# A two-layer graph kernel on one core: where the ones of a row are counted, and when the verdict on the inputs falls

## The reference: what is computed

```python
adj0 = A * (y @ y.T)                              # layer 0: neighbours of the same class
adj0 = adj0 / max(sum(abs(adj0), axis=1), 1e-12)
x = layernorm(x + 0.9 * (adj0 @ x) + 0.1 * h0)
sim = tanh(adj * adj) * (adj > 0)                 # layer 1: tanh(1) at every one
new_adj = top_350_of_each_row(sim)                # all of it where a row has at most 350 ones
feat = relu(new_adj @ (tanh(x @ W_proj + b_proj) @ W_gcn) + b_gcn)
out = layernorm(x + feat)
```

## Time and profile before

| | |
|---|---|
| median of 3 runs | 478.86 us (477.89 to 480.38) |
| profiled execution, its own time | 478.8 us |
| its span, first to last instruction | 477.0 us |
| PE busy | 449.3 us, 94% |
| DVE busy | 378.9 us, 79% |
| ACT busy | 262.7 us, 55% |
| transfers | 108.50 MB, 418 GB/s in layer 0, under 20 GB/s in layer 1 |

### The profile page before, as it was taken

One profiled execution on the slowest core, in us unless ns is written; L12 is line 12 of the kernel. 1 busy time (PEld: TensorE's weight loads), 2 busy tenths in 40 slices (PEclk: granted clock), 3 DMA queues, 4 the chain that ended last, 5 costly groups with the idle time before them and its releaser, 6 DMA issues.

```text
span 477.0 us, 15332 instructions
## 1 busy us (share of the span) xinstructions
PE 449.3 (94%) x5104; PEld 391.1 (82%) x5104; DVE 378.9 (79%) x1401; ACT 262.7 (55%) x353; POOL 159.5 (33%) x309
## 2 busy tenths in 40 slices
PE   3669999999999999999999999999999999999990
PEld 2448888989998899889998878888888888888880
DVE  5889999999999999999999866566566566566552
ACT  4988999999999999999999826300000000000000
POOL 3012544445555554444555431221221221221220
PEclk9988999999999999999999999999999999999996
DMA  8999999999999999999998000000000000000000
GB/s 267 406 419 418 402 419 393 384 416 417 414 416 416 421 418 422 420 419 421 419 415 326 8 0 1 19 11 17 17 11 17 17 11 17 17 11 17 17 18 10
DMA packets 28254, 108.50 MB, mean 227 GB/s; under 512 B 5401, under 2 KB 18226, under 8 KB 18226
## 3 DMA queue, kind: packets, MB, share of 16 engines
q1 hardware_dynamic: 28226, 108.14, 56.6%
HBM read 105.57 MB, written 2.56 MB: 227 GB/s over the span
## 4 chain that ended last, share of the span: by engine, by line
PE 88%; DVE 5%; DMA 2%; issue 2%; ACT 1%; POOL 1%; POOLq 0%; DVEq 0%; SPq 0%; ACTq 0%
PE acc L492 73%; PE words L443 8%; PE proj_acc L571 3%; PE feat_acc L555 2%; DMA a_rows<-in_adj_dram 2%; DVE a_bits L746 2%; PE xnt_acc L547 1%; DVE g_words L302 1%; POOL pack_half L373 1%; DVE turned L830 1%; ACT count_out L648 1%; DVE x_parts L775 0%; PE gram_acc L475 0%; DVE y_diag L760 0%; DVE same_class L850 0%
## 5 line engine op out<-in xcount | busy, mean ns | idle before, releaser
L492 PE MATMUL acc<-x_parts,turned 128*128 128x257 f16 (+1 forms) x1600 | 195.8, 277 | 0.7 <-DVE x_parts L775 0.7
L648 ACT ACTIVATE count_out<-a_rows,ones 128x2688 bf16<-128x2688 f32 (+1 forms) x80 | 190.0, 2375 | 0.5
L492 PEld LDWEIGHTS acc<-x_parts,turned 128*128 128x128 fp8e4 (+1 forms) x1600 | 157.0, 99 | 25.9 <-DVE x_parts L775 1.2
L492 PE MATMUL acc<-f_parts,turned 128*128 128x257 f16 (+1 forms) x1560 | 175.4, 273 | 0.0
L492 PEld LDWEIGHTS acc<-f_parts,turned 128*128 128x128 fp8e4 (+1 forms) x1560 | 151.2, 97 | 23.2 <-issue 0.4
L746 DVE TENSOR_SCALAR a_bits<-a_rows 128x2688 bf16<-128x2688 f32 (+1 forms) x80 | 116.7, 1459 | 3.3 <-DMA a_rows<-in_adj_dram 2.9
L830 DVE TENSOR_SCALAR turned<-a_words 128x320 uint16 (+1 forms) x305 | 66.9, 233 | 58.7 <-PE acc L492 58.4
L400 POOL TENSOR_TENSOR var_eps<-mean_var,consts 128x1 f32<-128x1 f32 x80 | 18.5, 231 | 272.6 <-DVE mean_var L1036 143.2
L403 POOL TENSOR_TENSOR rstd<-var_eps,consts 128x1 f32<-128x1 f32 x80 | 86.0, 1075 | 6.3
L830 DVE TENSOR_SCALAR turned<-same_class 128x320 uint16<-128x320 uint16 x313 | 71.2, 253 | 0.1
L443 PEld LDWEIGHTS words<-pack,a_bits 128*128 128x128 bf16 (+1 forms) x1600 | 53.6, 96 | 10.3 <-DVE a_bits L746 6.7
(11 more groups left out here) (109 smaller groups left out, 289.9 us busy)
## 6 DMA issues: line engine op xcount, KB each, us to landing
a_rows<-in_adj_dram SPq DMA_DIRECT2D x39, 1344.0 KB, 8.1
a_rows<-in_adj_dram SPq DMA_DIRECT2D x39, 1156.0 KB, 8.6
h_rows<-in_L_gnn_h_dram SPq DMA_DIRECT2D x39, 64.0 KB, 6.1
out_dram<-xn SPq DMA_DIRECT2D x39, 64.0 KB, 1.5
xs<-in_x_dram SPq DMA_DIRECT2D x3, 640.0 KB, 10.0
xs<-in_x_dram SPq DMA_DIRECT2D x1, 512.0 KB, 9.0
y_nat<-in_L_gnn_y_dram SPq DMA_DIRECT2D x1, 304.0 KB, 3.6
a_rows<-in_adj_dram SPq DMA_DIRECT2D x1, 84.0 KB
```

The lines of the kernel that those rows point to most:

```text
L492: mm = pe.matmul(acc[par][0:m, 0:PARTS], bits, parts[:, b, 0:PARTS], start=first and b == blocks[0], stop=last and b == blocks[-1])
L648: act.activation(count_out[0:m, 0:w], a_rows[par][h][0:m, 0:w], ACT.Relu, bias=ones[0:m, 0:1], scale=-HUGE, accum_out=col).then_inc(s_coun ...
```

## The change

1. `pack` gets a ninth column of ones. Packing a block of `a_bits` then gives 8 words and the number of ones. Results lie 10 apart (`PITCH`) in PSUM and in `a_words`, 9 of each 10 are copied by ACT. The readers of `a_words` on DVE (mask, unpack of layer 1) now read 8 of each 10.
2. `f_parts` loses its constant column: rows of 256 columns, 256 apart, and layer 1 multiplies 256 columns. `x_parts` keeps 257. The reading of `degree` in every block of layer 1 is gone.
3. The check changes: ACT sums all ones of a partition over the whole of `a_words` in one instruction behind its other checks; DVE sums `need` over the blocks and compares the two totals. These checks move to steps 3 and 4 of layer 1 on DVE (in `before`: step 39 and behind the last block).
4. PE's matmul of the verdict stands ahead of the products of the last row block, the flag is written in DVE's step NB, ahead of the last block's output.
5. Both paths share one block of code: no barrier between them. Each engine waits for the flag, loads it and branches. SP's wait for the stores moves behind its branch. Where the general path runs, the five engines meet at a semaphore first.

The core of the diff:

```diff
+    PITCH = WORDS + 2
-        pack = sb("pack", [P, WORDS], BF16)
+        pack = sb("pack", [P, WORDS + 1], BF16)
-        f_parts = sb("f_parts", [P, NB, PARTS + 1], F16)
-        a_words = sb("a_words", [P, NB, NB * WORDS], U16)
+        f_parts = sb("f_parts", [P, NB, 2 * F], F16)
+        a_words = sb("a_words", [P, NB, NB * PITCH], U16)
...
             steps(sp, store, 0)
-            sp.wait_ge(s_out[0], 16 * (NB // 2))
-            sp.wait_ge(s_out[1], 16 * (NB // 2))
...
-                    mm = pe.matmul(words[par][0:k, b * WORDS:(b + 1) * WORDS],
+                    mm = pe.matmul(words[par][0:k, b * PITCH:b * PITCH + WORDS + 1],
                                    a_bits[h][0:m, c:c + (k - 1) * d + 1:d], pack[0:m, :], start=True, stop=True)
...
             def multiply_blocks(n, par, m, parts, blocks, first=False, last=False):
+                cols = PARTS if parts is x_parts else 2 * F
                 for b in blocks:
                     bits = turned_at(n, par)[:, b, :].bitcast(F8)[:, 0:m]
-                    mm = pe.matmul(acc[par][0:m, 0:PARTS], bits, parts[:, b, 0:PARTS],
+                    mm = pe.matmul(acc[par][0:m, 0:cols], bits, parts[:, b, 0:cols],
                                    start=first and b == blocks[0], stop=last and b == blocks[-1])
...
+                if isinstance(t, int) and t == LAST:
+                    pe.wait_ge(s_good, CHECKS)
+                    pe.matmul(feat_acc[0:1, 0:1], verdict[:, :], ones[:, 0:1], start=True, stop=True)\
+                        .then_inc(s_sum, 1)
...
-                    act.activation(at(a_words, n, P), words[par][:, 0:NB * WORDS], ACT.Copy).then_inc(s_words, 1)
+                    act.activation(at(a_words, n, P).rearrange("p (b w) -> p b w", w=PITCH)[:, :, 0:WORDS + 1],
+                                   words[par][:, 0:NB * PITCH].rearrange("p (b w) -> p b w", w=PITCH)[:, :, 0:WORDS + 1],
+                                   ACT.Copy).then_inc(s_words, 1)
...
+            act.wait_ge(s_measured, 4)
+            act.activation(count_out[:, 0:NB * NB].rearrange("p (n b) -> p n b", b=NB),
+                           a_words[:, :, :].rearrange("p n (b w) -> p n b w", w=PITCH)[:, :, :, WORDS],
+                           ACT.Copy, accum_out=ones_in[:, :]).then_inc(s_measured, 1)
...
+            dve.memset(pack[:, WORDS:WORDS + 1], 1.0)
...
+            def check_sums():
+                dve.wait_ge(s_measured, 5)
+                done(dve.tensor_scalar(holds[:, 3, :], x_sums[:, :], 1.0, None, ALU.is_le))
+                done(dve.tensor_scalar(holds[:, 4, :], f_sums[:, :], 1.0, None, ALU.is_le))
+                done(dve.tensor_reduce(good[:, :], holds[:, :, :], AX.XY, ALU.min))
+                done(dve.tensor_tensor(surplus[:, :], ones_in[:, :], need_in[:, :], ALU.subtract))
+                done(dve.scalar_tensor_tensor(verdict[:, :], good[:, :], 1.0, surplus[:, :], ALU.subtract, ALU.add))
...
+            def words_at(n):
+                return at(a_words, n, P).rearrange("p (b w) -> p b w", w=PITCH)[:, :, 0:WORDS]
...
-                    dve.tensor_scalar(degree[0:m, bass.ds(t - 2, 1)], acc[par][0:m, 2 * F:PARTS], 0.5 / SCALE,
-                                      None, ALU.mult).then_inc(s_degree, 1)
...
+                if isinstance(t, int) and t == 3:
+                    check_counts()
+                if isinstance(t, int) and t == 4:
+                    check_sums()
+                if isinstance(t, int) and t == NB:
+                    dve.wait_ge(s_sum, 1)
+                    dve.tensor_scalar(flag[:, :], feat_acc[0:1, 0:1], 0.0, 0.0, ALU.is_equal, ALU.is_equal)\
+                        .then_inc(s_flag, 1)
...
+            pe.wait_ge(s_flag, 1)
             bad = pe.value_load(flag[0:1, 0:1], min_val=0, max_val=1)
             with pe.If(bad != 0):
+                pe.sem_inc(s_quit, 1)
+                pe.wait_ge(s_quit, 5)
...
+            sp.wait_ge(s_stored[0], 16 * (NB // 2))
+            sp.wait_ge(s_stored[1], 16 * (NB // 2))
```

More of the change, by code:

```diff
@@ L34, with packed_path @@
 PART_MAX = 32768.0
-def packed_path(nc, x, adj, h0, y, w_proj, b_proj, w_gcn, b_gcn, out, flag):
+def packed_path(nc, engines, sem, x, adj, h0, y, w_proj, b_proj, w_gcn, b_gcn, out, flag, s_flag, s_out):
     N, F = x.shape
@@ L52, in packed_path @@
     PARTS = 2 * F + 1
-    CHECKS = 11
+    CHECKS = 13
+    PITCH = WORDS + 2
     EARLY = NB - 4
@@ L58, in packed_path @@
     assert F == P and 0 < TAIL <= 2 * WORDS and C == BITS and FULL % 4 == 3 and FULL > FIRST
-    assert NB * WORDS <= 512 and NB % 4 == 0
+    assert NB * PITCH <= 512 and NB % 4 == 0
     def rows_of(t):
@@ L180, in packed_path @@
         zeros_in = sb("zeros_in", [P, 2 * NB])
-        degree = sb("degree", [P, NB])
+        ones_in = sb("ones_in", [P, 1])
+        need_in = sb("need_in", [P, 1])
+        surplus = sb("surplus", [P, 1])
+        verdict = sb("verdict", [P, 1])
         x_sums = sb("x_sums", [P, NB])
@@ L263, in packed_path @@
         s_passed = sem("s_passed")
-        s_degree = sem("s_degree")
         s_result = sem("s_result")
-        s_out = [sem(f"s_out{p}") for p in range(2)]
         s_good = sem("s_good")
         s_sum = sem("s_sum")
-        s_flag = sem("s_flag")
         def turned_at(n, par):
@@ L459, in _ @@
                 mm = pe.matmul(y_pack[b // Y_CUT][:, c:c + WORDS],
-                               y_masked[:, b, :], pack[:, :], start=True, stop=True)
+                               y_masked[:, b, :], pack[:, 0:WORDS], start=True, stop=True)
                 if b in (Y_CUT - 1, LAST):
@@ L603, in _ @@
             steps(pe, step1, 0)
-            pe.wait_ge(s_good, CHECKS)
-            pe.matmul(feat_acc[0:1, 0:1], good[:, :], ones[:, 0:1], start=True, stop=True)\
-                .then_inc(s_sum, 1)
         @engines.scalar
@@ L726, in _ @@
             for p in range(2):
-                dve.memset(words[p][:, LAST * WORDS:NB * WORDS], 0.0)
+                dve.memset(words[p][:, LAST * PITCH:NB * PITCH], 0.0)
             dve.memset(zeros_in[:, :], N / 2)
-            for a in (degree, x_sums, f_sums):
+            for a in (x_sums, f_sums):
                 dve.memset(a[:, :], 0.0)
             dve.memset(x_parts[:, :, 2 * F], SCALE)
-            dve.memset(a_words[:, LAST, LAST * WORDS:NB * WORDS], 0).then_inc(s_cleared, 1)
+            dve.memset(a_words[:, LAST, LAST * PITCH:NB * PITCH], 0).then_inc(s_cleared, 1)
             dve.memset(y_diag[:, :, :, :], 0.0).then_inc(s_yp_sb, 1)
             dve.wait_ge(s_pack, BITS)
-            dve.tensor_tensor(pack[:, :], pack_half[:, 0, :], pack_half[:, 1, :], ALU.add).then_inc(s_packs, 1)
+            dve.memset(pack[:, WORDS:WORDS + 1], 1.0)
+            dve.tensor_tensor(pack[:, 0:WORDS], pack_half[:, 0, :], pack_half[:, 1, :], ALU.add).then_inc(s_packs, 1)
             dve.tensor_reduce(in_half[:, :], pack_half[:, :, :], AX.X, ALU.max).then_inc(s_packs, 1)
@@ L762, in _ @@
             dve.wait_ge(s_yp_sb, TURN + 1)
-            dve.memset(words[1][:, LAST * WORDS:NB * WORDS], 0.0).then_inc(s_yp_sb, 1)
+            dve.memset(words[1][:, LAST * PITCH:NB * PITCH], 0.0).then_inc(s_yp_sb, 1)
             cast(0, 0, 0, 0)
@@ L782, in feature_ones @@
             def feature_ones():
-                dve.memset(f_parts[:, LAST, 0:2 * F], 0.0)
-                dve.memset(f_parts[:, :, 2 * F], SCALE).then_inc(s_cleared, 1)
+                dve.memset(f_parts[:, LAST, :], 0.0).then_inc(s_cleared, 1)
             k = [0]
@@ L940, in bits @@
                     if valid(t - 1):
-                        unpack(t - 1, odd, rows_of(t - 1), same_class[:, :], lo, hi)
+                        unpack(t - 1, odd, rows_of(t - 1), same_class[:, :].rearrange("p (b w) -> p b w", w=WORDS), lo, hi)
                 def begin(t_of, u, lo, hi):
                     if isinstance(t, int) and t == t_of:
-                        unpack(u + NB, u % 2, rows_of(u), at(a_words, u, P), lo, hi)
+                        unpack(u + NB, u % 2, rows_of(u), words_at(u), lo, hi)
                 begin(NB + 3, 1, 0, BITS // 2)
@@ L999, in bits @@
                     if valid(t) and (not isinstance(t, int) or t > 2):
-                        unpack(t + NB, par, rows_of(t), at(a_words, t, P), lo, hi)
+                        unpack(t + NB, par, rows_of(t), words_at(t), lo, hi)
                 bits(0, 2)
@@ L1155, in block_view @@
             return a[0:FULL * P, :].rearrange("(b p) f -> p b f", p=P)
-        block = ctx.enter_context(nc.Block())
         def row_range(t, m):
@@ L1462, in gnn_kernel, with sem @@
 def gnn_kernel(nc, x, adj, h0, y, w_proj, b_proj, w_gcn, b_gcn, out):
-    with nc.sbuf_tensor("flag", [1, 1], I32) as flag:
-        packed_path(nc, x, adj, h0, y, w_proj, b_proj, w_gcn, b_gcn, out, flag)
-        general_path(nc, x, adj, h0, y, w_proj, b_proj, w_gcn, b_gcn, out, flag)
+    with nc.sbuf_tensor("flag", [1, 1], I32) as flag, ExitStack() as sems, nc.Block() as engines:
+        def sem(name):
```

(5 more changed lines are left out.)

54 lines of the change are left out of this document (29 added, 25 removed).

## The result

| | before | changed |
|---|---|---|
| median, on one chip | 478.86 us (477.89 to 480.38, 5 runs) | 471.02 us (470.71 to 472.29, 5 runs) |
| ratio, 95% interval | | 0.984, 0.982 to 0.986 |
| profiled execution: time, span | 478.8, 477.0 us | 470.7, 468.9 us |

A forecast was written before the change was run, and what follows sets the result against it. PE was taken to bound both layers, in layer 0 with DVE and ACT close behind. From 478.8 us, -5.2 (tail), -5.0 (layer 1 products), +0.1 and +0.2 gave 468.9 us; range for 8 in 10: 467.2 to 473.4.

The forecast's parts named there:

- main case: Whole kernel: all four parts work as forecast, 468.9 us, own range 467.6 to 470.4; chance 0.72.
- rival of another late branch: End of the kernel: DVE's branch takes 3.85 us and delays the barrier, +2.6 us, 471.5 us; chance 0.11.
- signs of being wrong: Mask or unpack over 400 ns, layer 0 grown, or more than 0.5 us between the store's landing and the barrier.
- Part 1: The tail: all but the last store's landing and one barrier leaves the path, span ends at 471.8, -5.2 us.
- 470.1, if its branch stays short: End of the kernel: DVE's finish time in us, from output ready at 469.1, 0.9 for the flag, 0.07 for its branch.
- Part 2: Layer 1 products with 256 columns: 3.2 ns less each over 1560 products, -5.0 us.
- columns only: Layer 1: a product becomes only 0.42 ns shorter, -0.65 us, time 473.2 us; chance 0.12.
- Part 3: Layer 0: ninth packing column free on PE, ACT's copy and DVE's mask hidden; memsets at the start cost +0.1 us.
- rival that ended slower: Layer 1: DVE's unpack, reading 8 of each 10, loses the fast mode, 412 to 490 ns, time 482.9 us; chance 0.04.
- Part 4: Checks moved into layer 1 stay hidden; PE's verdict matmuls ahead of the last block cost at most +0.2 us.
- Needed only at some 309: Layer 1: the next block's unpack, queued on DVE behind the new sum's checks, is needed at some 309 us, hence hidden.
- 305.1: still hidden: Layer 1: ACT's new sum, expected done by 303.6 us, would at half speed end at 305.1 and still be hidden.

The follow-up runs named there:

- contiguous sum: Changed kernel, but ACT's layer 1 sum reads 1600 words side by side and the count of ones in adj leaves the verdict: 471.32 us, one execution.

## Why the prediction was right, and where it was not

**The range held, the main case did not.** The median, 471.02 us, lies in the range only because that was drawn over two rivals. It lies outside the main case's own range, 467.6 to 470.4, and next to the rival of another late branch (471.5), which had a chance of 0.11. Of the forecast's own signs of being wrong one came true: more than 0.5 us between the landing and the barrier. SP saw the landing at 467.4, and DVE came to the barrier at 468.6.

**Part 1, -5.2 us forecast, -3.9 measured.** One barrier, SP's landing, PE's branch hidden: all seen. The step that failed is the one on DVE, "470.1, if its branch stays short". The rival of another late branch came true, with two sizes off: the jump cost DVE 3.0 us and not 3.85, and it began at 465.6, 3.7 us behind the last product and not 4.0, so that 1.0 us showed and not 2.6. I had taken DVE's 67 ns as its price; the record of a branch on DVE doesn't hold the time to the next instruction, PE's does. Another 0.1 us is the landing, 5.4 us behind the last product for 5.3.

**Part 2, -5.0 forecast, -4.1 measured before the stall.** The mechanism was right, the term was too large: 3.2 ns a product, measured 2.58. It came from the row of matmuls of 256 columns at 28 us. By the trace's ns these are 108.7 apart, so the row was read well enough; a product of layer 1, with another operand type and adding up, takes 109.17, and that it would take the same was assumed. The rival "columns only" is refuted: even at a good pitch the column makes 0.8 ns and not 0.42, and the pitch 1.1 to 1.75. I had named the odd pitch, but not asked what it costs in layer 0, where it stayed.

**Part 3, +0.1 forecast.** Block 6.31, packing 25.2 ns, unpack 231 ns, mask 361 ns: right. So the rival that ended slower is refuted: DVE reads rows of 8 at a pitch of 10 as fast as contiguous ones in the unpack and 15 ns slower in the mask. The upper end that the prediction set for a slow read, 490 ns, comes from no row, and nothing here came near it. The -1.0 us in front of layer 1 was chance, as far as the runs show, and it hid as much of what the other parts fell short by.

**Part 4, +0.2 forecast, +1.0 measured.** Here stood the error of reasoning. "Needed only at some 309" was right as a time: PE needed the block at 307.9, in a layer that began 1.0 us earlier than in the trace of before. But it needed the end of its unpack, and left out were, behind ACT's sum, DVE's five instructions, 1.2 us, a pause of 0.35 and the unpack, 3.1 us between the instructions of the output: 304.09 + 1.2 + 0.35 + 3.1 = 308.7. The same sum on the prediction's two ends for ACT, 303.6 and 305.1, gives 308.3 and 309.8. So at 1.5 us the sum would have been hidden, as the run with the contiguous sum shows, and "305.1: still hidden" is the step that failed: ACT took 3.1 us, twice the proportion. PE's matmul of the verdict cost under 0.1 us.

In all: -3.9 - 4.1 + 1.0 - 1.0 = -8.0, the -8.1 of the span but for rounding, for a forecast of -9.9. The median came out 2.1 us above the forecast. The changed kernel run again, whose layer 1 began at 284.6 as in the trace of before, took 471.62 us, 2.7 above it.

## What to carry to other kernels

Try a pitch that is a multiple of 16 bytes for the rows of a matmul's moving operand: with one constant column at the end of a row of 256, the pitch of 516 bytes cost every product 1.75 ns over that of 528. A wait put into a busy queue is priced by what stands behind it down to the last instruction that the bounding engine needs, not to the next one in the queue. The cost of a taken branch is read from the instruction behind it, and a jump belongs where its engine has nothing left to do, as PE's does here.
